# A graph layer on one core: edge comparison before the q copy, and edge attributes as nine bf16 products

## What is computed

```python
def _L0_gnn_ref(x, edge_index, edge_attr, eW1, eb1, eW2, eb2, nW1, nb1, nW2, nb2):
    row, col = (edge_index[0], edge_index[1])
    edge_input = jnp.concatenate([x[row], x[col], edge_attr], axis=-1)
    h = jax.nn.silu(edge_input @ eW1 + eb1)
    m_ij = jax.nn.silu(h @ eW2 + eb2)
    agg = jax.ops.segment_sum(m_ij, row, num_segments=x.shape[0])
    node_input = jnp.concatenate([x, agg], axis=-1)
    update = jax.nn.silu(node_input @ nW1 + nb1) @ nW2 + nb2
    return x + update
edge_index = jnp.stack([src, dst])
x = _layernorm(x + _L0_gnn_ref(x, edge_index, edge_attr_16, ...), axis=-1)
```

## Time and profile before

| | |
|---|---|
| time, median of 3 runs | 1559.54 us (1555.54 to 1565.26) |
| time of the profiled execution | 1570.02 us, span 1568.2 us |
| plan, edge and node stage in the span | about 0 to 179, 179 to 1257, 1257 to 1568 us |
| mean granted TensorE clock | 0.89 of full |

### The profile page before, as it was taken

The page is one execution under the profiler, slowest core; times in us unless marked ns, Lnnn a source line. Parts: engine busy times, 40 slices in busy tenths (PEclk is TensorE's granted clock), DMA queues, the critical chain, the costliest instruction groups (busy, mean ns, idle before and its releaser), DMA issues.

```text
span 1568.2 us, 20795 instructions
## 1 busy us (share of the span) xinstructions
PE 1216.9 (78%) x6237; PEld 826.2 (53%) x6237; DVE 760.1 (48%) x2820; ACT 462.9 (30%) x846; POOL 1040.0 (66%) x1268
## 2 busy tenths in 40 slices
PE   3812587889888788888787977776777979999995
PEld 3811344455454445454444544444444579888884
DVE  8950343443444334344343433333333459888885
ACT  0000111122222222222222222212222247776774
POOL 8877466566665566465556566666666548898996
PEclk9996788799998889898989888888888979999997
DMA  9996333456566455656556555545454169999994
GB/s 335 413 411 244 87 113 103 123 177 182 165 181 185 145 165 177 177 152 184 167 165 174 160 152 151 167 140 178 152 158 136 52 222 407 409 410 407 408 411 160
DMA packets 183319, 333.46 MB, mean 213 GB/s; under 512 B 25647, under 2 KB 89695, under 8 KB 183204
## 3 DMA queue, kind: packets, MB, share of 16 engines
q1 hardware_dynamic: 136580, 211.68, 40.7%
q0 software_dynamic: 25024, 52.10, 11.0%
q10 hardware_dynamic: 21600, 68.32, 11.0%
HBM read 215.94 MB, written 116.06 MB: 212 GB/s over the span
## 4 chain that ended last, share of the span: by engine, by line
PE 42%; another core or an unknown queue 27%; DMA 8%; DVE 8%; issue 8%; ACT 3%; POOL 2%; SPq 0%; ACTq 0%; POOLq 0%; DVEq 0%
DMA ring<-table 7%; PE psum L737 6%; PE psum L665 6%; PE psum L708 5%; PE psum L706 5%; PE psum L688 4%; PE psum L710 4%; PE psum L719 4%; PE psum L752 3%; PE psum L696 2%; DVE work L909 2%; DMA edge_rows<-edges_dram 2%; PE psum L653 1%; POOL table L547 1%
## 5 line engine op out<-in xcount | busy, mean ns | idle before, releaser
L547 POOL DMA_INDIRECT table<-qs,pos x391 | 386.6, 989 | 344.1 <-DVE qs L1030 232.5
L504 POOL DMA_INDIRECT ring<-x_d,idx_src x391 | 398.8, 1020 | 124.6 <-issue 118.7
L987 DVE COPY work<-psum 128x512 f32<-128x512 f32 x98 | 67.8, 691 | 556.9 <-remote 275.8
L665 PEld LDWEIGHTS psum<-work,windows 128*128 128x128 f32 x980 | 177.7, 201 | 157.8 <-issue 140.5
L665 PE MATMUL psum<-work,windows 128*128 128x256 f32 (+1 forms) x980 | 199.1, 352 | 70.0 <-DVE work L996 55.2
L688 PE MATMUL psum<-xT_in,w_self 128*128 128x320 f32 x314 | 127.7, 491 | 122.6 <-ACT u_out L789 82.6
L737 PE MATMUL psum<-work,ring 128*128 128x80 f32 x1250 | 158.2, 281 | 26.0 <-DVE work L1050 21.4
L737 PEld LDWEIGHTS psum<-work,ring 128*128 128x128 f32 x1250 | 150.1, 197 | 35.3 <-issue 21.0
L708 PE MATMUL psum<-work,w_src 128*128 128x512 f32 x196 | 131.2, 756 | 46.6 <-DVE work L987 39.0
L795 ACT ACTIVATE work<-psum,b_e 128x512 f32<-128x512 f32 x98 | 67.4, 687 | 326.9 <-PE psum L710 162.6
L719 PE MATMUL psum<-work,w_e 128*128 128x512 f32 x196 | 124.4, 722 | 26.7 <-issue 13.7
(11 more groups left out here) (123 smaller groups left out, 1659.6 us busy)
## 6 DMA issues: line engine op xcount, KB each, us to landing
ring<-table SPq DMA_DIRECT2D x79, 528.0 KB, 10.8
table<-empty ACTq DMA_DIRECT2D x9, 4224.0 KB
edge_rows<-edges_dram SPq DMA_DIRECT2D x98, 384.0 KB
windows<-x_wide_d SPq DMA_DIRECT2D x98, 320.0 KB
xT_in<-xT_d SPq DMA_DIRECT2D x78, 320.0 KB
out<-windows ACTq DMA_DIRECT2D x78, 320.0 KB, 6.2
u_dram<-u_out SPq DMA_DIRECT2D x64, 320.0 KB
own_x<-x_d SPq DMA_DIRECT2D x48, 320.0 KB, 7.2
```

Source lines behind the costliest of these rows:

```text
L504: pool.indirect_dma_start(rows, None, x[:, :], bass.IndirectOffsetOnAxis(ap=idx[:, g * TILES + t:g * TILES + t + 1], axis=0)).then_inc(don ...
L547: pool.indirect_dma_start(table[:, :], bass.IndirectOffsetOnAxis(ap=pos[:, g * TILES + t:g * TILES + t + 1], axis=0), q[g % Q][:, t, :], None,
L665: last = nc.tensor.matmul(p_dst[:, tiles], window[g % WINDOWS][:, j, :], pick[g % 2][:, places], start=j == 1, stop=j == 4, skip_group_che ...
```

## The change

Three things.

1. In VectorE's loop `compare_edges(g+2)` stands ahead of `copy_q(g-1)`.
2. The attributes and their weights are each split into three bf16 parts (high, middle, low), and the product is made of nine bf16 products. `attr` now has 96 rows: three parts of 16 attributes, twice. `w_attr_hm` has the weights' high part against the first 48 rows and their middle part against the other 48, `w_attr_l` the low part against the first 48. So one float32 matmul (two MATMUL instructions) becomes two bf16 matmuls (one MATMUL instruction each).
3. The parts are made on the chip. Host code only lays the attributes out in batches of eight groups (128 rows of 512). SP loads a batch, VectorE splits it with four instructions (`split_attr`), SP stores the three parts twice to DRAM, and from there loads the 96 rows of each group. The first batch is split behind the one-hot loop of the plan, and its store and the first three loads stand ahead of the flag that SP reads before the edge stage. Later batches are loaded, split and stored at groups 0, 1 and 4 of the eight ahead of them. Eight small instructions at the plan's end split the weights.

POOL's instructions are the same as before.

```diff
+            def load_attr(g):
+                k, r = divmod(g, BATCH)
+                wait(sp, s_attr_out, 32 * (k + 1))
                 wait(sp, s_h_mm, g - ATTR + 1)
-                sp.dma_start(attr[g % ATTR][:], attrT[:, g * GROUP:(g + 1) * GROUP]).then_inc(s_attr[g % ATTR], 16)
+                rows = attr_dram[k, :, :, r * DE:(r + 1) * DE, :].rearrange("j i f e -> (j i) f e")
+                sp.dma_start(attr[g % ATTR][:], rows).then_inc(s_attr[g % ATTR], 16)
+            def store_attr(k):
+                sp.wait_ge(s_attr_split, 4 * (k + 1))
+                for j in range(2):
+                    sp.dma_start(attr_dram[k, j].rearrange("i p e -> p i e"), attr_parts[:]).then_inc(s_attr_out, 16)
+            def serve_attr(g):
+                k = g // BATCH + 1
+                if g < 0 or k >= BATCHES:
+                    return
+                if g % BATCH == 0:
+                    sp.wait_ge(s_attr_split, 4 * k)
+                    sp.dma_start(attr_left[:], attr_batches[k]).then_inc(s_attr_in, 16)
+                if g % BATCH == 4:
+                    store_attr(k)
...
-            for g in range(ATTR):
-                load_attr(g)
             sp.wait_ge(s_first, 1)
...
             sp.wait_ge(s_first_row, 16)
+            store_attr(0)
+            for g in range(ATTR):
+                load_attr(g)
             sp.wait_ge(s_fits_i, 1)
...
                     if g >= 0:
                         load_attr(g + 3)
+                    serve_attr(g)
                     serve_self(g)
...
+            pe.wait_ge(s_w_attr, 8)
             pe.wait_ge(s_before_tile, 1)
...
-                nc.tensor.matmul(p_h, w_attr[:], attr[g % ATTR][:], start=True, stop=False)
+                nc.tensor.matmul(p_h, w_attr_hm[:], attr[g % ATTR][:], start=True, stop=False)
+                nc.tensor.matmul(p_h, w_attr_l[0:PARTS, :], attr[g % ATTR][0:PARTS, :], start=False, stop=False)
...
+            def split_attr(k):
+                wait(dve, s_attr_in, 16 * (k + 1))
+                wait(dve, s_attr_out, 32 * k)
+                V.tensor_copy(attr_parts[:, 0, :], attr_left[:]).then_inc(s_attr_split, 1)
+                dve.wait_ge(s_attr_split, 4 * k + 1)
+                V.tensor_tensor(attr_left[:], attr_left[:], attr_parts[:, 0, :], ALU.subtract).then_inc(s_attr_split, 1)
+                dve.wait_ge(s_attr_split, 4 * k + 2)
+                V.tensor_copy(attr_parts[:, 1, :], attr_left[:]).then_inc(s_attr_split, 1)
+                dve.wait_ge(s_attr_split, 4 * k + 3)
+                V.tensor_tensor(attr_parts[:, 2, :], attr_left[:], attr_parts[:, 1, :], ALU.subtract).then_inc(s_attr_split, 1)
+            split_attr(0)
             V.tensor_tensor(reach[:], dst_max[:], dst_first[:], ALU.subtract).then_inc(s_plan, 1)
...
                 copy_xs(g + 1)
+                compare_edges(g + 2)
                 if g > 0:
                     copy_q(g - 1)
                 find_pos(g + 1)
-                compare_edges(g + 2)
+                if g % BATCH == 1 and g // BATCH + 1 < BATCHES:
+                    split_attr(g // BATCH + 1)
```

More of the change, by code:

```diff
@@ L57, in padded_edges, with gnn_kernel @@
     return (E + GROUP - 1) // GROUP * GROUP
-def gnn_kernel(nc, E, x, x_wide, xT, src_all, src_idx, dst_idx, dst_g, attrT, w1s, w1d, w1a, eb1, w2, eb2, nw1a, nb1, nw1b, nw2, nb2,
+def gnn_kernel(nc, E, x, x_wide, xT, src_all, src_idx, dst_idx, dst_g, attr_batches, w1s, w1d, w1a, eb1, w2, eb2, nw1a, nb1, nw1b, nw2, nb2,
                out):
     N = x.shape[0]
-    DE = attrT.shape[0]
+    DE = w1a.shape[0]
+    BATCHES, BATCH = attr_batches.shape[0], P // DE
+    PARTS, TWICE = 3 * DE, 6 * DE
     GROUPS = dst_g.shape[0]
@@ L87, in gnn_kernel @@
     u0_dram = nc.dram_tensor("u0_dram", (STORED, P, BLOCK), F32, kind="Internal").ap()
+    attr_dram = nc.dram_tensor("attr_dram", (BATCHES, 2, 3, P, GROUP), BF16, kind="Internal").ap()
     q_dram = nc.dram_tensor("q_dram", (P, D), F32, kind="Internal").ap()
@@ L131, in gnn_kernel @@
         xsT, xdT, hT, mT = ([work[:, (4 + 2 * k + s) * GROUP:(5 + 2 * k + s) * GROUP] for s in range(2)] for k in range(4))
-        attr = [sb(f"attr{s}", [DE, GROUP]) for s in range(ATTR)]
+        attr = [sb(f"attr{s}", [TWICE, GROUP], BF16) for s in range(ATTR)]
+        attr_left, attr_parts = sb("attr_left", [P, GROUP]), sb("attr_parts", [P, 3, GROUP], BF16)
         is_coarseT = [sb(f"is_coarseT{s}", [P, GROUP], F16) for s in range(2)]
@@ L163, in gnn_kernel @@
             worst, worst_all, fits = tmp("worst", [P, 1]), tmp("worst_all", [1, 1]), tmp("fits", [1, 1])
+            w_attr, w_sum = tmp("w_attr", [TWICE, D]), tmp("w_sum", [TWICE, D])
+            w_high, w_mid = tmp("w_high", [TWICE, D], BF16), tmp("w_mid", [TWICE, D], BF16)
+            is_first, is_second = tmp("is_first", [TWICE, 1]), tmp("is_second", [TWICE, 1])
             b_high, b_mid = tmp("b_high", [P, D], BF16), tmp("b_mid", [P, D], BF16)
@@ L223, in gnn_kernel @@
         s_scattered = [sem(f"s_scattered{s}") for s in range(Q)]
+        s_attr_in, s_attr_split, s_attr_out, s_w_attr = (sem(n) for n in ("s_attr_in", "s_attr_split", "s_attr_out", "s_w_attr"))
         s_src_turned, s_dst_turned, s_pick, s_xsT, s_xdT = (
@@ L374, in _ @@
             sp.dma_start(dst_i[:], dst_g.rearrange("g (t p) -> g t p", p=P)).then_inc(s_dst_i, 16)
-            for dst_sb, src_dram in ((w_src, w1s), (w_dst, w1d), (w_attr, w1a), (w_e2, w2), (w_agg, nw1b), (w_self, nw1a),
+            for dst_sb, src_dram in ((w_src, w1s), (w_dst, w1d), (w_e2, w2), (w_agg, nw1b), (w_self, nw1a),
                                      (w_out, nw2)):
                 sp.dma_start(dst_sb[:], src_dram).then_inc(s_weights, 16)
+            sp.dma_start(w_attr[:], w1a.unsqueeze(0).to_broadcast([6, DE, D])).then_inc(s_weights, 16)
+            sp.dma_start(attr_left[:], attr_batches[0]).then_inc(s_attr_in, 16)
             for dst_sb, src_dram in ((b_e1, eb1), (b_e2, eb2), (b_n1, nb1)):
@@ L977, in _ @@
                                    ).then_inc(s_b_parts, 1)
+            V.tensor_copy(w_high[:], w_attr[:]).then_inc(s_w_attr, 1)
+            V.tensor_scalar(is_first[:], row_f[0:TWICE, 0:1], PARTS - 0.5, None, ALU.is_lt).then_inc(s_w_attr, 1)
+            V.tensor_scalar(is_second[:], row_f[0:TWICE, 0:1], PARTS - 0.5, None, ALU.is_gt).then_inc(s_w_attr, 1)
+            dve.wait_ge(s_w_attr, 3)
+            V.tensor_tensor(w_attr[:], w_attr[:], w_high[:], ALU.subtract).then_inc(s_w_attr, 1)
+            V.tensor_scalar(w_sum[:], w_high[:], is_first[:, 0:1], None, ALU.mult).then_inc(s_w_attr, 1)
+            dve.wait_ge(s_w_attr, 5)
+            V.tensor_copy(w_mid[:], w_attr[:]).then_inc(s_w_attr, 1)
+            dve.wait_ge(s_w_attr, 6)
+            V.tensor_tensor(w_attr_l[:], w_attr[:], w_mid[:], ALU.subtract).then_inc(s_w_attr, 1)
+            V.scalar_tensor_tensor(out=w_attr_hm[:], in0=w_mid[:], scalar=is_second[:, 0:1], in1=w_sum[:], op0=ALU.mult,
+                                   op1=ALU.add).then_inc(s_w_attr, 1)
             dve.wait_ge(s_ids, 1)
@@ L1102, in by_block, with by_batch @@
         return rows
+    def by_batch(attr):
+        batch, de = P // attr.shape[1], attr.shape[1]
+        groups = -(-padded_edges(E) // (GROUP * batch)) * batch
+        rows = np.zeros((groups * GROUP, de), attr.dtype)
+        rows[:E] = attr
+        return rows.reshape(groups // batch, batch, GROUP, de).transpose(0, 1, 3, 2).reshape(groups // batch, P, GROUP)
     no_node = ((-(-N // BLOCK) * BLOCK) + BUCKET * np.arange(pads)).astype(src.dtype)
```

4 lines of the change are left out of this document (2 added, 2 removed).

## The result

The changed kernel took 1666.8 us (median of 4 runs, 1660.04 to 1675.08) beside 1557.91 us for the kernel before (1555.54 to 1565.26): a ratio of 1.069, with a 95% interval of 1.063 to 1.075. The forecast was 1518, and 1465 to 1595 the range. The change is 7% slower in this comparison, and later runs show another condition, in which the same two kernels tie at 1345 us.

What follows compares the result with a forecast made beforehand. Late TensorE signals and the half clock were taken to bound the edge stage. Terms of -72 - 36 + 54 + 2 + 5 + 5 = -42 us took 1570.0 to 1528; the median lies 10.5 lower: 1518 us, range 1465 to 1595.

Steps and rivals of the forecast that it cites:

- What bounds the kernel: Edge stage, 1078 us in 98 groups: late TensorE signals and the half clock behind them make a group cost 11 us.
- held signals: TensorE's matmul record is over but its semaphore comes microseconds later, while POOL issues indirect DMAs without a pause.
- The attribute product: TensorE, edge stage: two bf16 matmuls for one float32 save 0.73 us a group, 72 us in all (59 to 73).
- The lower of the two values: Attribute product on TensorE: saving of 0.43 us a group at the full clock, where the other value was 0.62.
- the prediction's shares of the two clocks: TensorE in the edge stage: 0.76 of the time at the full clock, 0.24 at half.
- The comparison ahead of the q copy: VectorE's loop: TensorE's waits for `pick` go, saving 36 us (0 to 36); the later q copy costed at nothing.
- What comes back: Edge stage: part of TensorE's relief returns as more late signals and half clock, +54 us (0 to 76).
- the slope: Middle against late groups: 1.3 us more POOL work goes with 0.91 us more time, 0.7.
- VectorE's split: Casts and subtractions for the attribute parts: nothing in the loop, +2 us for the first batch in the plan.
- more DMA: Attribute loads and stores, 192 KB more a group, 19 MB in all: +5 us, between nothing and 20.
- the way in: Start of the edge stage: first group 15 to 25 us later behind SP's first stores, mostly hidden, +5 us.
- Slower: POOL loses its pauses: Rival, edge stage: later q copy makes POOL issue without pause, middle groups at the late pace; 1595 us, chance 0.18.

Runs made afterwards that it cites:

- h_no_gather: Kernel before without the gathers of source rows for groups 28 to 97, in the held condition: 1259.81 us.
- h_after_no_gather: Changed kernel without the gathers of source rows for groups 28 to 97, in the held condition: 1218.55 us.
- e_pick_first: Kernel before with only the comparison's two instructions that write `pick` moved ahead of the q copy: 1607.03 us, ratio 1.014.
- e_attr: Changed kernel with VectorE's old order, so the attribute part without the moved comparison: 1574.1 us, ratio 0.997 to the kernel before.
- e_order: Kernel before with only the comparison moved ahead of the q copy: 1688.75 us, ratio 1.066.
- h_pool_late: Kernel before with POOL's scatter also waiting for VectorE's comparison of the edges four groups ahead, in the held condition: 1696.18 us, ratio 1.086.
- e_pick_last: Kernel before with the comparison's six other instructions ahead of the q copy and the two that write `pick` left at the end: 1630.71 us, ratio 1.029.
- h_gap: Kernel before with a rest of POOL (four small fills, each waited for) after every four indirect transfers, held condition: 1620.21 us, ratio 1.036.
- h_gap_after: Changed kernel with a rest of POOL (four small fills, each waited for) after every four indirect transfers, held condition: 1622.51 us, ratio 1.036.

## Why the prediction was wrong, point by point

**What bounds the kernel.** The reading of held signals was right, and right for this condition alone: the stage is as long as late signals make it. That the kernel before also runs in 1345 us, with POOL as its bound, no row of its one trace could show.

**The attribute product.** The two products take 0.63 us from 632.19 to 632.82, and 0.31 for one. The saving at the full clock is 1.05 - 0.63 = 0.42 us, not 0.62; the row of the node stage was a poor measure for them. The lower of the two values was right, and the estimate of 0.43 from the four passes that the Trainium skill (FP8 and Floating Point Precision, section TensorE Precision Notes) gives a float32 product agrees with the trace and with the 0.42 us a group between `h_no_gather` and `h_after_no_gather`. At the half clock the two take 1.10 us from 652.97 on, so the saving is 0.90, not 1.14. With the prediction's shares of the two clocks that is 0.54 us a group, 52 us of relief, where 72 stood in the sum and 59 was its lower end.

**The comparison ahead of the q copy.** TensorE's wait for `pick` went as forecast. No run shows it to be worth anything: `e_pick_first` removes it and is 1.4% slower, and `e_attr`, with twice as much of it, is no slower.

**The failed step.** "I cost it at nothing; the cover is POOL's slack of 11.28 - 8.9 = 2.4 us a group", it says. The q copy's 2.7 us was costed at nothing for the forecast, and it is the whole loss: 1.066 in `e_order`, 1.086 when POOL alone is made late. The slack was an average. POOL has it in pauses at certain places, and its waits for q grew from 232.5 to 327.3 us and those of `copy_xs` for late signals from 275.8 to 448.4. In the changed kernel, `e_order` and `h_pool_late` the later start closes two turns of four up against the next two, so that runs of 8 become runs of 16, and a signal of TensorE that falls into such a run comes up to 10 us behind its record (634.80 to 644.70), while TensorE idles and drops to the half clock. That the longer runs are what carries the loss is argued from these three; `e_pick_last` loses 2.9%, and its trace has none of 16 between 500 and 900 us.

**What comes back.** The step is uneven: half of the 76 us that the slope gives would be 38, and the 54 in the sum are half of the whole relief of 108. In `e_attr`, which has the relief and the small costs of splitting but not the new order, 6 us of some 52 are left. So most came back or went into those costs, which no run separates. The direction was right; the size was too small.

**VectorE's split, more DMA, the way in.** `e_attr` has all of them and is not slower, so together they are at most what the relief covers. The first SiLU of the edge stage came 26 us later (157 instead of 131), but POOL's gather behind it went at 173.0 instead of 169.5 and the third group's SiLU at 184.4 instead of 186.1: hidden, as forecast. The 24 transfers of POOL beside the split's instructions took 1.02 us on average and the others of the stage 0.98, with a single one at 1.51, so no lock worth a term in the sum shows there either.

**The rivals.** "Slower: POOL loses its pauses" had the right part of the program, the right sign and the right point of decision (a middle group over 11.4 us; it is 12.4), and a chance of 0.18. Its price of 1595, or 1628 at most, was too low: it took the late groups of before, 12.19 us, as the worst, and the middle groups of the change went to 12.4. (The 1595 is also not what its words give: with half the relief kept, 36 or 54 us, it would be 1592 or 1574.) POOL didn't lose its pauses: it waited 327 us for q where it was 232, in fewer and longer waits.

**What was shown and what not.** Shown: the order alone costs the time; POOL's later start alone does too; in the free condition nothing of it exists. With runs of four the later q costs nothing, by the pair with rests and, where POOL isn't the bound, by one run of each of two kernels. Not settled: why a signal is late in the one condition and not in the other, how long a run or how short a rest decides it, and how the later start costs time in the middle of `e_pick_last`, where no run of 16 forms. Signals also arrive in the middle of a run (638.38 and 644.70 above), so a run delays them rather than stops them.

## What to carry to other kernels

Slack that is an average over a group doesn't cover a delay: look at where the pauses lie and at what a later start pushes together, above all on an engine that issues DMAs in bursts. Delay the suspected engine alone by one wait, as `h_pool_late` does: it costs a line and separates the start of the burst from everything else that a reordering moves. And run the kernel before again on each occasion: a tuned order can be tuned to a condition.

## What the runs showed of the hardware

- One kernel, unchanged, took 1343 to 1349 us in two sets and 1554 to 1586 on the four other occasions, and did both on chip number 11. The changed kernel's gather (L535) has a mean of 1028 ns in both conditions; its two traces differ in the 448.4 us of waits of `copy_xs` for late signals against none, and in the clock, 0.81 in the edge stage against 0.94.
- In the held condition VectorE waited 43.9 us for a signal of TensorE, which came 37.8 us behind its record, while POOL issued 112 indirect DMAs in a row (`h_no_gather`). With 1.8 us from one turn of four to the next, one such wait of 0.8 us was left from 200 us on in `h_gap`, and two of 4.8 us together in `h_gap_after`.
- A bf16 matmul with 512 columns took 0.31 us among float32 ones, start to start, where two with 640 columns together took 0.27 in the node stage.
